# The position-table products of a head, and their copies, in the last two quarters of the step instead of the first two

## What is computed

```python
q = split_heads(x @ Wq + bq)          # 32 images, 16 heads, 512 tokens, 16 channels a head
k = split_heads(x @ Wk + bk)
v = split_heads(x @ Wv + bv)
scores = einsum('bhqd,bhkd->bhqk', q, k) / scale
pos_k, pos_q = ...                    # projections of 128 relative positions
c2p = take_along_axis(einsum('bhqd,hpd->bhqp', q, pos_k), bucket(i - j), axis=-1) / scale
p2c = swapaxes(take_along_axis(einsum('bhkd,hpd->bhkp', k, pos_q), bucket(j - i), axis=-1)) / scale
probs = softmax(scores + c2p + p2c)
ctx = einsum('bhqk,bhkd->bhqd', probs, v)
return ctx @ Wo + bo
```

## Time and profile before

| what | value |
| --- | --- |
| time, median of 3 runs | 4945.38 us (4916.66 to 4955.33) |
| the profiled execution's own time | 4949.42 us |
| its span, first to last instruction | 4947.7 us |
| TensorE matmul busy | 4503.2 us, 91% |
| VectorE busy | 3496.9 us, 71% |
| ScalarE busy | 2689.6 us, 54% |
| GpSimd busy | 1862.1 us, 38% |
| moved by DMA | 1540.36 MB, mean 311 GB/s |
| mean granted TensorE clock | 0.958 of 2.4 GHz |

### The profile page before, as it was taken

How to read it: one execution, slowest core, us unless ns; L and a number is a source line. 1 busy time by engine, 2 the same in 40 slices (tenths; PEclk the granted TensorE clock), 3 DMA queues, 4 the chain that set the end, 5 groups by cost and what they waited for, 6 DMA issues and landing times. The chain is left out here.

```text
span 4947.7 us, 91672 instructions
## 1 busy us (share of the span) xinstructions
PE 4503.2 (91%) x29893; PEld 3225.0 (65%) x30324; DVE 3496.9 (71%) x9091; ACT 2689.6 (54%) x5075; POOL 1862.1 (38%) x4431
## 2 busy tenths in 40 slices
PE   6999999599999999999999999999999997883699
PEld 5777777366666666666666666666666665773566
DVE  3333333388888888888888888888888886776511
ACT  1222222277777777777667676767676664441111
POOL 1222222244444444444444444444444442330032
PEclk9999999799999999999999999999999998885599
DMA  5888888899999999999999999999999996662033
GB/s 169 279 285 275 278 286 276 292 382 382 379 388 387 390 378 375 373 378 376 369 376 377 376 372 373 378 373 383 371 377 368 373 369 205 215 207 82 3 96 82
DMA packets 684020, 1540.36 MB, mean 311 GB/s; under 512 B 50211, under 2 KB 286163, under 8 KB 683475
## 3 DMA queue, kind: packets, MB, share of 16 engines
q1 hardware_dynamic: 674646, 1523.26, 85.1%
q0 software_dynamic: 6144, 8.52, 1.0%
q10 hardware_dynamic: 2816, 3.41, 0.2%
HBM read 753.82 MB, written 781.21 MB: 310 GB/s over the span
## 5 line engine op out<-in xcount | busy, mean ns | idle before, releaser
L984 ACT ACTIVATE a_probsT<-a_ps_m_t 128x512 f32<-128x512 f32 x2048 | 1223.8, 605 | 828.0 <-PE a_ps_m_t L924 828.0
L1046 DVE CUSTOM_DVE_ANT_1 a_scored<-a_ps_m_s,a_bias 128x512 f32<-128x512 f32 x2048 | 1393.1, 680 | 311.0 <-PE a_ps_m_s L915 302.0
L924 PE MATMUL a_ps_m_t<-a_ident,a_scored 128*128 128x128 f32 x8192 | 1257.7, 276 | 0.5 <-ACT a_probsT L984 0.5
L924 PEld LDWEIGHTS a_ps_m_t<-a_ident,a_scored 128*128 128x128 f32 x8192 | 935.2, 141 | 433.2 <-DVE a_scored L1053 427.8
L978 ACT ACTIVATE a_skew_in<-a_ps_m_tab 128x512 f32<-128x512 f32 x2048 | 1124.2, 612 | 163.8 <-DMA d_skew<-a_skew_in 126.9
L1053 DVE TENSOR_SCALAR a_scored<-a_scored,a_top_of 128x512 f32<-128x512 f32 x2048 | 1075.1, 545 | 0.0
L870 POOL TENSOR_SCALAR_AFFINE_SELECT a_bias<-a_bias 128x128 f32<-128x128 f32 (+2 forms) x2560 | 1004.8, 419 | 35.1
L861 POOL COPY a_bias<-a_high 128x128 f32<-128x128 f32 (+1 forms) x1024 | 358.4, 380 | 1679.8 <-DMA a_bias<-d_skew 1679.8
L915 PE MATMUL a_ps_m_s<-a_ident,a_bias 128*128 128x128 f32 x5120 | 895.7, 273 | 22.1 <-issue 0.7
L901 PE MATMUL a_ps_m_tab<-a_tabs,a_stack 128*128 128x256 bf16 x4096 | 711.5, 276 | 159.9 <-ACT a_skew_in L978 87.4
L915 PEld LDWEIGHTS a_ps_m_s<-a_ident,a_bias 128*128 128x128 f32 x5120 | 690.1, 141 | 177.5 <-issue 1.4
(11 more groups left out here) (195 smaller groups left out, 3566.8 us busy)
## 6 DMA issues: line engine op xcount, KB each, us to landing
d_skew<-a_skew_in SPq DMA_DIRECT2D x512, 1024.0 KB, 9.5
a_bias<-d_skew SPq DMA_DIRECT2D x512, 896.0 KB, 8.6
a_stack<-d_stack SPq DMA_DIRECT2D x256, 512.0 KB, 9.0
p_xt<-in_xT SPq DMA_DIRECT2D x31, 2048.0 KB, 10.4
d_stack<-p_extra SPq DMA_DIRECT2D x64, 512.0 KB, 3.2
d_ctx<-a_ctx_sb SPq DMA_DIRECT2D x128, 256.0 KB, 9.9
d_stack<-p_part_q SPq DMA_DIRECT2D x64, 384.0 KB, 2.8
d_stack<-p_part_k SPq DMA_DIRECT2D x64, 384.0 KB, 3.4
```

Source lines behind the costliest of these rows:

```text
L924: mm = pe.transpose(m_t[:, k % 2, t * P:(t + 1) * P], scored[:, hh % SCORED, t, k * P:(k + 1) * P], ident[:])
L984: nc.scalar.activation(turned_at(hh // GH, hh % GH, k), m_t[:, k % 2], ACT.Exp, scale=SCALE).then_inc(turned, 1)
L1046: nc.vector.tensor_tensor_reduce(split(scored[:, hh % SCORED, t]), split(m_s[:, t % 2]), extra, 1.0, -3.0e38, ALU.add, ALU.max, top_of[:, ...
```

## The change

In both engines' step the condition `t < 2` becomes `t >= 2`, and the part numbers are counted from there: quarter three has parts 0 and 1, quarter four parts 2 and 3. Instructions, sizes, counts and semaphores are the same. The order in SyncE's, GpSimd's and VectorE's queues is unchanged, and so is the code ahead of the first step and behind the last.

```diff
--- before.py
+++ after.py
@@ TensorE, body of a step @@
                         if not early(b, hh, TURN):
                             turn(n - TURN, (hh - TURN) % NH, t)
-                        if t < 2 and not (last and m >= NH):
-                            for part in (2 * t, 2 * t + 1):
+                        if t >= 2 and not (last and m >= NH):
+                            for part in (2 * t - 4, 2 * t - 3):
                                 tables(n + LEAD, b + m // NH, m % NH, part)
```

## The result

The changed kernel takes 4882.38 us, the median of 4 runs (4875.07 to 4887.73), beside 4939.41 us of the kernel before in 4 runs (4916.66 to 4955.33). The ratio is 0.9887, with a 95% interval of 0.9844 to 0.9930: faster by 1.1%. I had forecast 4980 us, in a range of 4885 to 5055.

A forecast was written before the change was run, and what follows sets the result against it. It took TensorE as nearly the limit before 1700 us and the DMA queue after. +13, +10 to +16, +5 (context copy) and 2 us (stage ends) made about +33 on 4949: 4982, rounded to 4980 us, range 4885 to 5055.

The forecast's parts named there:

- the clean step: TensorE's time for one head in attention, apart from waits outside the step's own order: 6.02 us against 5.91, +0.11.
- the last copy's end: ScalarE's last table copy of a head: ends 7.42 us into the step instead of 5.36, 2.06 us later.
- the fill's wait: VectorE's table fill waiting for GpSimd: up from 91.4 us, in well over half of the heads.
- ScalarE's wait for landed writes: ScalarE waiting for a table write to land before refilling its staging buffer: 91.6 us before, forecast to go down.
- after 1700 us the DMA queue is the limit: Attention after 1700 us, some 390 heads: DMA-bound at 375 GB/s, 6.235 us a head.
- the pace of 6.26 after 1700 us: Time per head in later attention, from the five-head loop: +0.025 to +0.04 us a head, +10 to +16 us in all.
- 0.16 above the clean step: Attention before 1700 us, some 120 heads: the old gap kept, so 6.18 us a head against 6.07, +13 us.
- The order and spacing of the DMAs among themselves therefore stay: SyncE's queue: the later table writes slide the whole DMA pattern against the compute, with order and spacing unchanged.
- W + R: Landing times of a table's write and read, 9.5 + 8.6 = 18.1 us, perhaps shrinking by some tenths.
- the five-head loop: Last copy, write, read, GpSimd, VectorE's fill, then scores: 31.3 us instead of 29.2, against a budget of 31.2.
- Rival 2: TensorE's table stall goes away; the queue then holds 6.05 us a head: 4875 us, chance 0.15.
- Rival 1: The table's journey becomes the bound at VectorE's fill if W + R stays above 18.0: +85 us, 5035 us, chance 0.32.

The follow-up runs named there:

- a part per quarter: Changed kernel with one table part and its copy in each quarter instead of two in quarters three and four: 4852.21 us, ratio 0.9870 to the kernel before.
- the held write: Kernel before, with SyncE holding each table write until VectorE has finished the last scores of the step's head: 4871.90 us, ratio 0.9899.
- the third half: Kernel before with a third staging half for the tables and three score buffers instead of four: 5001.86 us, ratio 1.0166.
- the queue alone: Kernel before plus an extra stage issuing attention's DMAs without compute, fixed number in flight: 406 to 408 GB/s from four; a second run had 357 and 360.
- cap: Kernel before, each table write, table read or stack load issued only once the fourth last of these has landed: 4926.29 us, ratio 0.9997.
- the light hold: Kernel before, each table write held only until VectorE's third add of the step's head: 4886.38 us, ratio 0.9914.
- two parts in quarters two and three: Changed kernel with its table parts and copies moved to quarters two and three: 4923.49 us, ratio 1.0013 to the kernel before.
- the long hold: Kernel before, each table write held until VectorE's first add of the next head: 5005.98 us, ratio 1.0169.
- the clock: Kernel before plus an extra stage issuing attention's DMAs without its compute, timed by ScalarE copies, reads tied to landed writes: 381 GB/s sinking to about 350.

## Why the prediction was wrong

Right, by its own steps: the clean step (6.02 forecast, 6.02 measured, with 0.38 of stall where I had 0.42); the last copy's end, 7.42 forecast, 7.32 measured; the fill's wait grown, in well over half of the heads; ScalarE's wait for landed writes down. These were the compute's parts, worked out from the positions of single instructions.

The step that failed is the reading of what bounds the kernel: "after 1700 us the DMA queue is the limit", at 375 GB/s. I took a rate that I saw for the most that the queue can do. It did 385 in the changed kernel, 389 in one with a part per quarter, 408 alone. From it followed the pace of 6.26 after 1700 us (measured 6.07; over some 390 heads 74 us). The "0.16 above the clean step" for the rest was carried over without a reason (measured 0.03 before 1700 us, 0.05 after). What makes up the 0.16 isn't shown: the held write, at 6.05 us a head, still stands 0.14 above the clean step of its order, 5.91. Both go the same way, and with them the forecast of +33 us became a gain.

"The order and spacing of the DMAs among themselves therefore stay" failed too. Most reads are issued when their write lands (SyncE waits for it at 365 of 369 before, at 292 of 379 after). So the distance from a write to the next read is about the write's landing less the pace: 9.6 - 6.2 = 3.4 us before, 7.7 - 6.1 = 1.6 after. I let W + R shrink by "some tenths"; it shrank by 2.0 us, all but 0.1 of it in the write, and paid for the 2 us by which the tables leave later. That is why the five-head loop, forecast as just closed, cost at most 0.05 us a head.

Rival 2 had the sign and nearly the size (4875 us), for another reason: the step didn't fall to 5.69, and TensorE's stall stayed. Rival 1's fill did wait, but W + R was 16.2, not above 18.0. (Its 0.16 us over 512 heads are 82 us, not 85.)

That issuing the writes later is enough for such a gain is shown by the held write: its compute is that of the kernel before, only the writes are issued 1.4 us later, and it has the changed kernel's landing (7.6 us), rate (386 GB/s) and time. That the change works by the same path is inferred from these three. That taking ScalarE's wait away brings nothing is shown by the third half. That a slow condition can arise with no engine computing is shown by the queue alone (357 and 360 GB/s). Why a write that is issued early goes with slower transfers is not shown. It isn't a number of more than four in flight (cap), and neither the tie nor depth is needed (357 GB/s with three in flight). Nor is lateness the whole rule: the light hold of 0.3 us gained 0.9%, two parts in quarters two and three, about 1 us later, nothing. Across most kernels the rate falls with the landing of writes (7.6 and 7.7 us: 386 and 385 GB/s; 8.1: 389; 9.0: 383; 9.4: 377; 9.6: 375; 10.8: 374), which goes along with it and may be its effect; the long hold (6.6 us: 370), where ScalarE waits for landed writes again, breaks the row. This stays open.

## What to carry to other kernels

A DMA share of 1.0 and a rate that matches the pace don't prove that the queue is at its limit: compare the rate with its best stretch in the same trace, and with the transfers alone. When writes stand in line for half of their time, try to issue them later before you issue them earlier or add a buffer. A wait put on the issuing queue alone costs a line or two and tells whether a compute order matters for itself; read in the trace how far it moved the issue, for here one such wait moved nothing. When the same rule gives two rates in two runs (377 and 357 GB/s), no rule is proven by one of them. Here one part per quarter (4852 us) beat both kernels.

## What was unexpected in the hardware

- The same transfers in the same sizes had two rates, about 386 and 375 GB/s, and changed from one to the other within one execution (at about 1700 us in the kernel before), with the DMA share between 1.01 and 1.02 in both.
- One more buffer made the kernel 1.7% slower; one more wait made it 1.0% faster.
- Transfers tied as the kernel ties them started at 381 GB/s and sank within 60 us to about 350 under the clock; with four in flight they did 404. Untied, three in flight did 377 in one run and 357 in another.
